# Self-attention of a decoder block with the weight products made on the chip, and the probabilities divided at the residual addition

## The reference

```python
x_norm = (x - mu) / sqrt(var + 1e-5) * gamma + beta
q = x_norm @ qkv[:, :256]; k = x_norm @ qkv[:, 256:512]; v = x_norm @ qkv[:, 512:]
scores = where(causal, q @ k.T / 16, -inf)
out = softmax(scores) @ v @ o_proj + x
x1 = layernorm(x + out)          # then cross-attention, then the experts
```

## Time and profile before

| | |
|---|---|
| median of 3 runs | 1806.1 us (1800.71 to 1807.99) |
| profiled execution | 1804.36 us, of which the span of its instructions is 1802.4 us |
| busy share of the span | PE 82%, DVE 73%, POOL 62%, ACT 39% |
| mean granted TensorE clock | 0.906 of full |
| attention phase | until about 1090 us |

### The profile page before, as it was taken

How to read it: one execution, slowest core, us unless ns; L and a number is a source line. 1 busy time by engine, 2 the same in 40 slices (tenths; PEclk the granted TensorE clock), 3 DMA queues, 4 the chain that set the end, 5 groups by cost and what they waited for, 6 DMA issues and landing times. The chain is left out here.

```text
span 1802.4 us, 34145 instructions
## 1 busy us (share of the span) xinstructions
PE 1475.3 (82%) x9600; PEld 1233.7 (68%) x9600; DVE 1319.6 (73%) x3879; ACT 694.7 (39%) x1462; POOL 1109.3 (62%) x1090
## 2 busy tenths in 40 slices
PE   3679999999999899999999855779999999992000
PEld 2568888888888787888888744567777777771000
DVE  3458888888888888888888843147777765553898
ACT  3235444545453444444443412124444444441221
POOL 3328676767676667677776641027777777774444
PEclk8789999999999999999999977579999999996555
DMA  5861212121212112121212117976655556642886
GB/s 197 287 201 50 84 49 77 54 79 51 76 56 74 56 63 69 53 79 47 85 47 71 45 70 230 256 214 191 188 187 185 184 182 189 190 120 99 294 298 241
DMA packets 161421, 237.36 MB, mean 132 GB/s; under 512 B 28044, under 2 KB 135578, under 8 KB 156836
## 3 DMA queue, kind: packets, MB, share of 16 engines
q1 hardware_dynamic: 127636, 160.73, 29.2%
q0 software_dynamic: 27648, 69.28, 10.4%
q10 hardware_dynamic: 6032, 6.13, 1.0%
HBM read 127.47 MB, written 116.93 MB: 136 GB/s over the span
## 5 line engine op out<-in xcount | busy, mean ns | idle before, releaser
L1347 POOL DMA_INDIRECT expert_out_scratch<-y,target x320 | 319.1, 997 | 225.5 <-issue 107.4
L484 POOL DMA_INDIRECT slot_scratch<-xrow x256 | 272.2, 1063 | 187.8 <-DVE xrow L1100 111.6
L1438 ACT ACTIVATE x_turned<-bank_x 128x512 f32<-128x512 f32 x176 | 105.1, 597 | 281.1 <-PE bank_x L1377 281.0
L523 PE MATMUL bank_c<-wq_w,x1t 128*128 128x512 f32 x768 | 193.2, 403 | 15.4 <-DVE q_work L942 11.7
L1417 PE MATMUL bank_y<-dp,inter_t 64*128 (+1 forms) x704 | 205.7, 414 | 0.0
L1396 PE MATMUL bank_g<-gu,x_turned 128*128 (+1 forms) x1408 | 195.6, 284 | 0.0
L669 PE MATMUL bank_d<-wo_w,o2t 128*128 128x256 f32 x1536 | 193.4, 286 | 2.0 <-DVE o2t L858 2.0
L669 PEld LDWEIGHTS bank_d<-wo_w,o2t 128*128 128x128 f32 x1536 | 187.6, 192 | 3.1 <-DVE o2t L858 2.7
L1616 DVE COPY y<-bank_y 128x512 f32<-128x512 f32 x160 | 110.6, 691 | 97.1 <-PE bank_y L1417 97.1
L429 POOL TENSOR_TENSOR q_rs<-q_ve,minus_half 128x8 f32<-128x8 f32 x64 | 137.4, 2147 | 71.3 <-DVE q_ve L933 67.6
L523 PEld LDWEIGHTS bank_c<-wq_w,x1t 128*128 128x128 f32 x768 | 142.3, 190 | 56.6 <-DVE q_work L942 21.0
(11 more groups left out here) (232 smaller groups left out, 3074.0 us busy)
## 6 DMA issues: line engine op xcount, KB each, us to landing
x_rows<-slot_scratch SPq DMA_DIRECT2D x320, 136.0 KB
rows<-expert_out_scratch SPq DMA_DIRECT2D x32, 1152.0 KB, 5.6
slot_scratch<-zeros SPq DMA_DIRECT2D x18, 1088.0 KB, 11.8
gu<-in_gate_up SPq DMA_DIRECT2D x11, 768.0 KB, 12.5
expert_out_scratch<-y,target POOLq DMA_INDIRECT x320
token_row_scratch<-xrow SPq DMA_DIRECT2D x32, 136.0 KB, 1.8
x_rows<-token_row_scratch SPq DMA_DIRECT2D x16, 272.0 KB
dp<-in_down SPq DMA_DIRECT2D x22, 192.0 KB, 13.7
```

The source lines that it names most:

```text
L484: nc.gpsimd.indirect_dma_start(out=slot_d[:, :], out_offset=bass.IndirectOffsetOnAxis(ap=xrow[slot][:, SLOT8 + k:SLOT8 + k + 1].bitcast(U3 ...
L523: last = nc.tensor.matmul(target, left[a][:, c, :], right(b, c), start=(n == 0 and c == 0), stop=(n == len(PASSES) - 1 and c == C - 1))
L1347: nc.gpsimd.indirect_dma_start(out=y_d[:, :], out_offset=bass.IndirectOffsetOnAxis(ap=target[s % 8][:, j:j + 1], axis=0), in_=y[s % 4][:, ...
L1438: nc.scalar.activation(xt[s % 2][:, :, :, :].rearrange("p j c n -> p (j c n)"), bank_x[:, s % 2, :], ACT.Copy).then_inc(sig["x_copied"], 1)
```

## The change

The weights of query and key are multiplied with each other once on the chip, and so are those of value and output: the scores are `xn (Wq Wk^T) xn^T`, and the output `P (xn (Wv Wo))`. Per tile, the projection now gives 512 columns in all (`xn Wq Wk^T` and half of `xn Wv Wo`), two transposes are left instead of four, the other side of the scores is the full-precision transposed input `xnf` (a new copy by ScalarE), the probabilities go into their product unscaled, and that one product of 256 columns gives the output directly, straight into `x1_add`, where it is multiplied by the reciprocal of the sum and added to the input. The sum is half of what it was, so the norm's epsilon is a quarter. `copy_v`, `copy_self_out`, `self_output` and the division of the probabilities go. `x_low` now subtracts from `xnf` in SBUF instead of from PSUM. The order of the remaining stages stays.

Before the pipeline comes `fuse`: twelve transposes, three copies by ScalarE and eight fp32 matmuls (sixteen records) of 256 columns on TensorE, after which the high and low parts of 1024 columns are made from PSUM. `wq` is sent for when the products are made. ScalarE issues its small loads at the start, `o_proj` first.

```diff
-        qkv_w = [sb(f"qkv_w{n}", [P, C, 3 * D], F32R) for n in (HI, LO)]
+        qkv_w = [sb(f"qkv_w{n}", [P, C, 2 * D], F32R) for n in (HI, LO)]
@@ SyncE
-            sp.wait_ge(sig["qkv_lo"], 1)
+            sp.wait_ge(sig["fused_made"], 1)
             sp.dma_start(q_work[:, :].rearrange("p (c n) -> p c n", c=C), split3(wq)).then_inc(sig["wq_loaded"], 16)
@@ TensorE
-                product(bank_a[:, 1, :], xnt, lambda b, c: qkv_w[b][:, c, 0:2 * D]).then_inc(sig["qk_projected"], 1)
-                product(bank_a[:, 0, 0:D], xnt, lambda b, c: qkv_w[b][:, c, 2 * D:3 * D])\
-                    .then_inc(sig["v_projected"], 1)
+                product(bank_a[:, 1, :], xnt, lambda b, c: qkv_w[b][:, c, :]).then_inc(sig["qk_projected"], 1)
             def self_transpose(t):
                 pe.wait_ge(sig["qk_copied"], t + 1)
-                pe.wait_ge(sig["v_copied"], t + 1)
-                for c in range(2 * C):
+                for c in range(C):
@@
-                    last = nc.tensor.matmul(bank_a[:, 1, 0:P], qkt[:, c, :], qkt[:, C + c, :], start=(c == 0),
+                    last = nc.tensor.matmul(bank_a[:, 1, 0:P], tt[:, c, :], xnf[:, c, :], start=(c == 0),
@@
-                pe.wait_ge(sig["self_probs"], t + 1)
+                pe.wait_ge(sig["self_exp"], t + 1)
@@
             def self_attend(t):
                 pe.wait_ge(sig["self_pt_copied"], t + 1)
-                for c in range(C):
-                    last = nc.tensor.matmul(bank_b[:, 0, c * P:(c + 1) * P], v[:, c * P:(c + 1) * P], p1t[:, :],
-                                            start=True, stop=True)
-                last.then_inc(sig["self_out"], 1)
-            def self_output(t):
...
+                nc.tensor.matmul(bank_b[:, 0, 0:D], p1t[:, :], v, start=True, stop=True).then_inc(sig["self_proj"], 1)
@@
-                at(c, self_output)
@@
+            def fuse():
+                pe.wait_ge(sig["qkv_loaded"], 16)
+                for n, target in enumerate((bank_c[:, 0, :], bank_c[:, 1, :], bank_d[:, 0, :])):
+                    for k in range(C):
+                        for c in range(C):
+                            last = nc.tensor.transpose(target[:, k * D + c * P:k * D + (c + 1) * P],
+                                                       qkv_stage[:, c, n * D + k * P:n * D + (k + 1) * P], identity[:, :])
+                    last.then_inc(sig["fused_turned"], 1)
+                pe.wait_ge(sig["fused_copied"], 3)
+                pe.wait_ge(sig["o_loaded"], 16)
+                for c in range(C):
+                    for k in range(C):
+                        nc.tensor.matmul(bank_d[:, c, 0:D], turned[0][:, k, c * P:(c + 1) * P], turned[1][:, k, :],
+                                         start=(k == 0), stop=(k == C - 1))
+                    for k in range(C):
+                        last = nc.tensor.matmul(bank_d[:, c, D:2 * D], turned[2][:, k, c * P:(c + 1) * P], o_w[:, k, :],
+                                                start=(k == 0), stop=(k == C - 1))
+                last.then_inc(sig["fused_made"], 1)
@@ ScalarE
             def x_high(t):
+                copy("xn_full", flat(xnf[:, :, :]), bank_a[:, 0, 0:D], "xn_transposed", t + 1)
                 copy("xn_hi", flat(xnt[HI][:, :, :]), bank_a[:, 0, 0:D], "xn_transposed", t + 1)
@@
-                at(b, copy_v)
-                at(b, copy_self_out)
-            copy("qkv_hi", flat(qkv_w[HI][:, :, :]), q_work[:, 0:C * 3 * D], "qkv_loaded", 16)
+            act.dma_start(o_w[:, :, :], split3(o_proj)).then_inc(sig["o_loaded"], 16)
...
+            copy("qkv_hi", flat(qkv_w[HI][:, :, :]), flat(bank_d[:, :, :]), "fused_made", 1)
@@ VectorE
-                low("xn_lo", flat(xnt[LO][:, :, :]), bank_a[:, 0, 0:D], flat(xnt[HI][:, :, :]), "xn_hi", t + 1)
+                low("xn_lo", flat(xnt[LO][:, :, :]), flat(xnf[:, :, :]), flat(xnt[HI][:, :, :]), "xn_hi", t + 1)
@@
                 nc.vector.reciprocal(p1_rec[:, :], p1_sum[:, :]).then_inc(sig["self_recip"], 1)
-                dve.wait_ge(sig["self_recip"], t + 1)
-                nc.vector.tensor_scalar_mul(p1n[:, :], p1[:, :], p1_rec[:, :]).then_inc(sig["self_probs"], 1)
@@
-                nc.vector.scalar_tensor_tensor(h1[:, :], x_res[:, :], 2.0, bank_b[:, 0, 0:D], ALU.mult, ALU.add)\
+                dve.wait_ge(sig["self_recip"], t + 1)
+                nc.vector.scalar_tensor_tensor(h1[:, :], bank_b[:, 0, 0:D], p1_rec[:, :], x_res[:, :], ALU.mult, ALU.add)\
                     .then_inc(sig["h1_done"], 1)
```

More of the change, by code:

```diff
@@ L257, in flat @@
             return a.rearrange("p a b -> p (a b)")
+        qkv_stage = q_work[:, 0:C * 3 * D].rearrange("p (c n) -> p c n", c=C)
+        turned = [q_work[:, (3 + n) * 2 * D:(4 + n) * 2 * D].rearrange("p (k n) -> p k n", k=C) for n in range(3)]
         half = HEADS // 2
-        SMALL = 9
+        SMALL = 8
         LAG = 5
@@ L751, in copy_qk @@
                 copy("qk_copied", qk[:, :], bank_a[:, 1, :], "qk_projected", t + 1)
-            def copy_v(t):
-                copy("v_copied", v[:, :], bank_a[:, 0, 0:D], "v_projected", t + 1)
             def copy_qkt(t):
-                copy("qkt_copied", flat(qkt[:, :, :]), bank_a[:, 0, :], "qk_transposed", t + 1)
+                copy("qkt_copied", flat(tt[:, :, :]), bank_a[:, 0, 0:D], "qk_transposed", t + 1)
             def copy_self_probs(t):
                 copy("self_pt_copied", p1t[:, :], bank_b[:, 0, 0:P], "self_pt", t + 1)
-            def copy_self_out(t):
-                copy("self_ot", flat(o1t[:, :, :]), bank_b[:, 0, 0:D], "self_out", t + 1)
             def x1_high(t):
```

38 lines of the change are left out of this document (16 added, 22 removed).

## The result

| | before | after |
|---|---|---|
| median of 10 runs, us | 1808.0 | 1825.4 |
| the profiled execution, us | 1804.4 | 1822.6 |
| its span, us | 1802.4 | 1820.5 |
| mean granted clock over the span | 0.906 | 0.900 |

The changed kernel takes 1.0101 times as long as the one before, with a 95% interval from 1.0073 to 1.0128. Two of the ten executions of the changed kernel, of 2919 and 3644 us, are in a slower state and outside the ratio; without them the median is 1825.0. 1828 was forecast, with a range from 1802 to 1842. The time is close, and its reasons are not: the clock, from which 24.4 us were to come (22.9 in the filled pipeline and 1.5 in the draining), cost 7.3 (1.0 and 6.3), and the filling of the pipeline, put at 3.5, cost 10. That the two errors nearly cancel is luck.

The account below looks back on a forecast made before the run. A loop through TensorE, VectorE and GpSimd sets the 29.8 us period, with the removed work beside it. Terms -1.2 - 1.4 + 13.5 + 9.4 + 3.5 + 1.5, less some 2, give +23: 1828 us, range 1802 to 1842.

Parts of the forecast that it names:

- the clock: Filled pipeline: idler TensorE falls to half clock in about six steps of ten; +13.5 us first half, +9.4 second.
- the draining: End of the attention phase: a step loses its `self_output` and probably its clock; +1.5 us (0 to +3).
- the filling of the pipeline: Before the first steps: making the weight products delays the first store of x1; +3.5 us, ends +1 and +8.
- The loop: First half: `query_transpose` 1 still waits for GpSimd's `scale_queries`, so TensorE's saved 1.9 us gives 0.08 a step, -1.2.
- The division of the probabilities: Second half, VectorE: without it the first query bias comes 0.27 us earlier; -3.5 us, at most -1.4 left with falls.
- Rival 1: Filled pipeline: the clock holds and the time hardly changes, 1803 to 1812, say 1806 us; chance 0.22.
- The 13.2 us of work behind the landing: Filling: transposes, copies, products and weight parts between `qkv`'s arrival and the first projection; 13.2 us.
- The landing of `qkv`: Filling: ScalarE's loads, now beside `qkv`, make it arrive 1 to 2.5 us later.
- +4.5 at `wo`: Filling: high part of `wo` comes 4.5 us later, with the first projection 6.5 later.
- steps with other pauses: Steps near the middle and the ends, whose pauses differ; some 2 us taken off the sum.
- The second rival: Steps: TensorE itself is the bound, 1757 us, or VectorE disturbs GpSimd less, 1796; chance 0.09 in both forms.
- the third's dear filling: Filling costs +8 us or more, with clock falls in nearly each step, up to 1848 us; chance 0.07.

Follow-up runs that it names:

- e4: Changed kernel with two useless 256-column products on TensorE where `self_output` stood: 1823.0 us, ratio 1.0063 to the kernel before.
- e9: Changed kernel with GpSimd scaling only four of eight query heads, in a slower series: 1990.7 us, ratio 0.9913 to the kernel before.
- e10: Kernel before with GpSimd scaling only four of eight query heads, in a slower series: 1995.7 us, ratio 0.9964 to it unedited.
- e1: Changed kernel with `x_low` subtracting from PSUM again instead of SBUF: 1819.3 us, ratio 1.0048 to the kernel before.
- e2: Changed kernel with ScalarE's small loads issued behind its copies of the turned weights: 1823.6 us, ratio 1.0078 to the kernel before.
- e3: Changed kernel without making the weight products, `qkv`'s first 512 columns used instead (wrong result): 1811.0 us, ratio 1.0007 to the kernel before.
- e12: Changed kernel with `x_low` reading PSUM, small loads issued later and key scaling on ScalarE, slower series: 1988.4 us, ratio 0.9908 to the kernel before.
- e8: Kernel before with the key scaling moved from GpSimd to ScalarE, in a slower series: 2004.3 us, ratio 0.9948 to it unedited.

## Why the prediction came out as it did

**The loop: right.** `query_transpose` 1 waits 1.26 us for GpSimd (1.2 to 1.5 was said), `chosen` takes 1.32 (about 1.3), and the work gone from TensorE moved no step (1.6 us by the busy time, where 1.9 was worked out). Even the 0.08 us a step, in sum -1.2, is not there: 5.53 before and after. e4 shows that TensorE's time is free, and e9 beside e10 that the leg is GpSimd's after the change and was not before it.

**The division of the probabilities: wrong.** It was costed at -3.5 in the second half, for the first query bias was to come 0.27 us earlier. The step that failed is that VectorE had nothing else to wait for. `cross_sum` now waits 0.41 us for ScalarE's exponential, on the way to that bias, and the biases still run back to back. The L901 that was removed had been work under the cover of a wait; what was late next stood on ScalarE, and its timeline I had not read there.

**The clock: wrong in its place, and mis-sized.** A fall in six steps of ten, +22.9, was forecast. In 28 steps of its trace there is one fall of 3.4 us that wasn't there before, and the one near the middle is 6.8 long instead of 3.4; together they cost 1.0 us. The failing step is the size of what is left for TensorE. A window over the new step, to put beside the two with which I compared it:

```profile
452.14:457.67 5.53, 3.97 (x27) 3.34 (x27) 4.78 (x14) 3.19 (x7) 5.45 (x5) 1.00 0.00 0
```

3.97 us of 5.53 are busy, where 5.5 less 1.9 had given 3.6. The neighbour that kept its clock had 3.54 of 5.45 and was the nearer one; I decided by the presence of `self_output` instead. e4 with `self_output`'s stand-in and the changed kernel without it both keep the clock in the filled pipeline, so its presence decides nothing there. Rival 1 described the filled pipeline: the clock holds.

The Trainium skill ("TensorE: Matmul & The Clock Gate", section "Why this matters for your kernels") warned, of gaps, of longer ones only, and for all but one of the steps away from the middle the trace bears it out. That one it doesn't foresee: the fall at 366.6 stands behind the same pauses as the other steps have, none longer than 1.28 us:

```profile
366.02 1.52 PE L600 MATMUL bank_c<-identity,q_work 128*128 128x128 f32 x8 [1.28 <-POOL q_work L458]
```

Nor does it foresee the fall at 1011.7, behind pauses of 0.71, 0.53 and 1.09 us, nor those of the slower series, one of them (e10, 0.59 from 392 to 394 us) right behind a pause of 2.31. There the kernel before fell more often than the changed one, the opposite of what was forecast for less work on TensorE.

**The draining: right in its kind, mis-sized.** +1.5 (0 to +3) was forecast for a lost clock, and it is +6.3. The fall was expected as long as the one in the trace, 3.4 us; it lasted 17.1, over `cross_score`, the whole output projection and the next queries. It is in after, e1, e2 and e3, each time 17.1 us in the same step, and in e4 it is not at this place. In the slower series only e9 of the five changed kernels has a fall there, of 13.7 us. Why a fall lasts 3.4 us at one place and 17.1 at another is open.

**The filling: right in its kind, mis-sized by 6.4.** +3.5 with ends of +1 and +8; measured +9.9 at the store of x1 (45.48 to 55.35) and +10.0 at the third step. Over all kept traces the store is at 43.9 to 45.5 with the kernel before and at 53.8 to 56.7 with the unedited products. The 13.2 us of work behind the landing are sound: 17.1 were measured to the first projection, and 3.85 of them are the slow `x_low`. Two other terms are at fault. The landing of `qkv` was put 1 to 2.5 us later; it is 4.7 later (e2). And `x_low` was let off with the sentence that GpSimd only issues scatters there. That is so in the filled pipeline. In the filling GpSimd makes the low part of `wk` and `wv`, 4.50 us of it, and the conflict that I had just weighed for `chosen` struck there, for 3.85 (e1). The forecast's +4.5 at `wo` for +6.5 at the first projection was sound in proportion: +10.3 at `wo` (42.53 us) for +13.6. And nearly all of that arrived at the store, as was said.

So the forecast had -2.6 for the steps (measured +0.3), +22.9 for the clock in them (1.0), +3.5 for the filling (10.0), +1.5 for the draining (6.3) and -2 for steps with other pauses; the measured ones make 17.6 of the 18.1 us between the two traces. Two errors of opposite sign met: an idle TensorE that was feared in the wrong place, and a filling that was priced from the view of the filled pipeline. That 1825 lies near 1828 is luck; with the clock term right and the rest as it stood, the forecast would have been near 1806, 19 us too low. The second rival's 1757 or 1796 needed a bound that isn't there; the third's dear filling came about, without the falls.

**What would have made it faster**, in the first series: e3 says that without the filling's cost the time is that of the kernel before (1.0007), and by the rows e1 and e2 together can give back most of it. The two together didn't run there, and no version that beats the kernel before was found there. In the slower series e12 does, by 0.9% (0.6 to 1.3). But the kernel before with the same key edit (e8) is 0.5% faster too (0.2 to 0.8), and the two intervals overlap, so how much of e12's gain is owed to the fused weights is not shown.

## What to carry to other kernels

Work taken from a busy engine is worth what the loop through the other engines lets it be: look for the instruction at which two engines arrive together, and cost the edit by the one that isn't shortened. Work that is done once to save work in each step is paid in the filling, where other engines are doing other things than in the filled pipeline, so read that stretch row by row for each new instruction, each load's neighbours and each operand's place. Whether a stretch loses the clock can't be told from which work is missing in it: here one kind of step kept it 26 times and lost it once with the same pauses. Take more than two neighbours from the trace, and look first at the last steps, where the work is thinnest.

## What the runs showed of the hardware

- One VectorE instruction of 256 columns took 0.42 us with an input in PSUM (e1) and 4.27 with both in SBUF (after), under a GpSimd instruction of 4.5. `chosen` takes 0.62 where GpSimd's instruction ends 0.54 us behind its start, and 1.32 where it ends 1.25 behind.
- TensorE kept 2.4 GHz over 26 steps with pauses such as 0.58, 0.30 and 1.26 us within 5.5 us and lost it once in such a step, for 3.4 us (after, 366.6). It lost it for 17.1 us after 0.71, 0.53 and 1.09 within 5.65 (after, e1, e2, e3).
- ScalarE's small loads on another queue moved the landing of the first weights from 9.9 to 14.2 us (e2).
- The same program took 1808 to 1811 us in two series and 2009 to 2014 in two others. Single instructions took the same time in both (4.50 and 4.49 us, and 4.27, among them); in the slower ones VectorE waited up to 3.3 us in its second residual addition, and the clock of the first half fell four to nine times instead of none to two.
